# Reordering the emptying steps of a fused RWKV and FP4 feed-forward kernel: two rounding chains interleaved on VectorE

## What is computed

```python
attn = _rwkv_scan(r, k, v, w)                      # state = state*w + k v^T, out = state r
y = attn * g @ W_o.T
x = _layernorm(x + _layernorm(y) * ln_gamma + ln_beta)       # first two norms
def fp4_quant_dequant(x):                          # per block of 16
    scale = max(max(abs(xb)) / 6, 1e-12)
    return _GRID[searchsorted(_MID, abs(xb / scale))] * sign(xb) * scale
gate, up = fp4_linear(x, w_gate), fp4_linear(x, w_up)
h = silu(gate) * up                                # 704 hidden features
x = _layernorm(x + fp4_linear(h, w_down))          # third norm
```

## Time and profile before

| | us |
|---|---|
| median of 3 runs | 567.41 (565.97 to 568.02) |
| the profiled execution, its own time | 568.91 |
| its span | 567.00 |
| busy: PE / DVE / POOL / ACT | 520.9 / 508.8 / 286.1 / 260.0 |

### The profile page before, as it was taken

How to read it: one execution, slowest core, us unless ns; L and a number is a source line. 1 busy time by engine, 2 the same in 40 slices (tenths; PEclk the granted TensorE clock), 3 DMA queues, 4 the chain that set the end, 5 groups by cost and what they waited for, 6 DMA issues and landing times.

```text
span 567.0 us, 14892 instructions
## 1 busy us (share of the span) xinstructions
PE 520.9 (92%) x5169; PEld 453.7 (80%) x5169; DVE 508.8 (90%) x1535; ACT 260.0 (46%) x614; POOL 286.1 (50%) x439
## 2 busy tenths in 40 slices
PE   2769789899999999999999999999999999988775
PEld 1657568788888898988888888888988888867764
DVE  7998577999999999999999999999999999889983
ACT  3426454455444455445455544445544545432231
POOL 3246443445565555555554555555655545556232
PEclk9978789999999999999999999999999999999999
DMA  7300000000000000000000000000000000000001
GB/s 212 126 1 2 11 11 10 1 22 20 20 20 20 23 10 12 21 21 20 20 21 21 20 20 20 22 20 4 18 21 21 10 11 11 13 0 21 10 10 32
DMA packets 14046, 13.14 MB, mean 23 GB/s; under 512 B 2576, under 2 KB 13712, under 8 KB 13968
## 3 DMA queue, kind: packets, MB, share of 16 engines
q1 hardware_dynamic: 13968, 12.13, 7.0%
HBM read 7.93 MB, written 4.19 MB: 21 GB/s over the span
## 4 chain that ended last, share of the span: by engine, by line
issue 47%; POOL 40%; PE 5%; DVE 4%; ACT 2%; POOLq 1%; DMA 0%; ACTq 0%; DVEq 0%
POOL scores L410 11%; POOL rstd L392 11%; POOL hq L462 8%; POOL nmr L404 4%; POOL shift L435 3%; POOL xb L448 2%; DVE mix L1233 1%; POOL xq L419 1%; PE bank L794 1%; ACT scores L589 1%; PE bank L919 1%; PE bank L891 1%; PE bank L971 1%; PE bank L743 0%; PE bank L862 0%
## 5 line engine op out<-in xcount | busy, mean ns | idle before, releaser
L589 ACT COPY scores<-bank 128x512 f32<-128x512 f32 x128 | 68.3, 593 | 74.2 <-PE bank L794 74.2
L462 POOL TENSOR_TENSOR hq<-late,h_scale 128x704 f32<-128x704 f32 x31 | 43.2, 1392 | 96.4 <-DVE late L1092 96.4
L971 PE MATMUL bank<-down_t,hq_t 128*128 128x256 f32 x384 | 88.2, 379 | 0.9 <-ACT hq_t L665 0.8
L410 POOL TENSOR_SCALAR_AFFINE_SELECT scores<-scores 128x512 f32<-128x512 f32 x128 | 80.6, 666 | 11.2 <-ACT scores L589 11.2
L1233 DVE SCALAR_TENSOR_TENSOR mix<-shift,mu,x_t 128x128 f32<-128x128 f32 x256 | 80.9, 364 | 1.3 <-POOL shift L435 1.3
L971 PEld LDWEIGHTS bank<-down_t,hq_t 128*128 128x128 f32 x384 | 71.6, 190 | 9.6 <-issue 1.0
L419 POOL TENSOR_TENSOR xq<-x_grid,x_scale 128x256 f32<-128x256 f32 x32 | 19.9, 620 | 113.7 <-DVE x_grid L1092 113.7
L392 POOL TENSOR_TENSOR rstd<-veps,neg_half 128x1 f32<-128x1 f32 x96 | 65.2, 688 | 18.1 <-DVE veps L1180 18.0
L855 PE MATMUL bank<-gu_hi,xq_hi 128*128 128x352 f32 x256 | 71.2, 359 | 2.6 <-DVE late L1297 2.6
L891 PE MATMUL bank<-mix,proj_t 128*128 128x128 f32 x512 | 65.2, 281 | 0.1
L891 PEld LDWEIGHTS bank<-mix,proj_t 128*128 128x128 f32 x512 | 60.2, 193 | 3.5 <-issue 1.3
(11 more groups left out here) (130 smaller groups left out, 1145.1 us busy)
## 6 DMA issues: line engine op xcount, KB each, us to landing
x_tok<-in_L_attn_x_dram SPq DMA_DIRECT2D x32, 128.0 KB, 2.3
out_dram<-late_down SPq DMA_DIRECT2D x32, 128.0 KB, 1.7
late_down<-in_L_ffn_w_down_dram SPq DMA_DIRECT2D x1, 704.0 KB, 8.3
late<-in_L_ffn_w_gate_dram SPq DMA_DIRECT2D x1, 640.0 KB, 4.6
late<-in_L_ffn_w_up_dram SPq DMA_DIRECT2D x1, 640.0 KB, 6.9
scores<-in_L_attn_W_r_dram SPq DMA_DIRECT2D x1, 256.0 KB, 4.5
scores<-in_L_attn_W_v_dram SPq DMA_DIRECT2D x1, 256.0 KB, 4.6
scores<-in_L_attn_W_g_dram SPq DMA_DIRECT2D x1, 256.0 KB, 4.8
```

What stands on the lines that cost most here:

```text
L410: g.affine_select(out=a, in_=a, compare_op=ALU.is_ge, fill=0.0, base=0, pattern=[[0, 4], [1, P]], channel_multiplier=-1).then_inc(s_masked, 1)
L462: g.tensor_tensor(blocks(hq[:, t.c % 2, 0:HID], nb), blocks(h_grid, nb), per_block(h_scale, nb), ALU.mult).then_inc(hq_ready, 1)
L589: s.copy(scores[:, t.c % 2, 4 * q:4 * q + 4, :], src).then_inc(s_moved, 1)
L971: mm = t_.matmul(B_PA[:, 0:C], hq_t[:, t.c % 2, j], down_t[:, j], start=(j == 0), stop=(j == NH - 1))
```

## The change

Only the emptying steps' lists change, and one wait. On VectorE the x chain's links now stand between the h chain's, two or three places behind, and `gated(0)` moves from behind the norms to a place behind the sixth link of the h chain. Its wait is loosened to match: it asked for all seven links of the tile ahead, and now asks for four, since the fourth is the last that reads `hid`. `norm3` and the state update move back a little. On GpSimd, in emptying steps, `xq` moves from the end of the list to the place right behind `hq`, the second norm's rstd and nmr follow it, and the third norm's come last.

```diff
--- before.py
+++ after.py
@@ -461,6 +461,11 @@
                     nb = HID // BLK
                     g.tensor_tensor(blocks(hq[:, t.c % 2, 0:HID], nb), blocks(h_grid, nb),
                                     per_block(h_scale, nb), ALU.mult).then_inc(hq_ready, 1)
+                if drain:
+                    scale_x(tile(5), general)
+                    t = tile(4)
+                    if t is not None:
+                        rstd_of(t, 1, general)
                 t = tile(7 + ffn)
                 if t is not None and drain:
                     rstd_of(t, 2, general)
@@ -475,9 +480,9 @@
                                         per_block(h_scale[:, half * nb:(half + 1) * nb], nb), ALU.mult
                                         ).then_inc(last_ready, 1)
                 t = tile(4)
-                if t is not None:
+                if t is not None and not drain:
                     rstd_of(t, 1, general)
-                if not general:
+                if not general and not drain:
                     scale_x(tile(5), general)
                 if general:
                     scale_x(tile(4), general)
@@ -1291,7 +1296,7 @@
                     if t5 is None:
                         return
                     if i == 0:
-                        wait(dve, hquant_step, t5.count(QN, 0))
+                        wait(dve, hquant_step, t5.count(QN, 4 - QN))
                     wait(dve, gu_done, t5.count(2, i + 1))
                     wait(dve, sig_ready, t5.count(2, i + 1))
                     v.tensor_tensor(hid[:, i * HH:(i + 1) * HH], sig_h[:, i], B_UP[:, 0:HH], ALU.mult
@@ -1409,33 +1414,36 @@
                     norm1(0)
                     hgrid(1)
                     norm1(1)
+                    xgrid(0)
                     hgrid(2)
                     norm1(2)
+                    xgrid(1)
                     centred()
+                    xgrid(2)
                     low_x()
                     hgrid(3)
                     residual()
+                    xgrid(3)
+                    hgrid(4)
+                    xgrid(4)
                     gate_heads()
-                    hgrid(4)
                     if t2 is None:
                         add_x1()
+                    hgrid(5)
+                    xgrid(5)
+                    gated(0)
                     norm2(0)
-                    hgrid(5)
+                    hgrid(6)
+                    norm2(1)
                     norm3(0)
-                    norm2(1)
-                    hgrid(6)
+                    xgrid(6)
+                    norm2(2)
                     norm3(1)
-                    norm2(2)
+                    next_state(0)
                     norm3(2)
-                    next_state(0)
-                    gated(0)
+                    next_state(1)
                     last_grid(0)
-                    xgrid(0)
-                    next_state(1)
-                    xgrid(1)
                     next_state(2)
-                    for k in range(2, QN):
-                        xgrid(k)
                     gated(1)
                     last_grid(1)
                     return
```

## The result

The changed kernel takes 570.02 us (median of 6 runs, 569.52 to 571.15) beside 567.10 us of the kernel before (6 runs on the same chip): a ratio of 1.0048, with a 95% interval of 1.0033 to 1.0064. On the 567.41 us from which the prediction started that is 570.1, between 569.3 and 571.0. The forecast was 569.4, in a range of 567.4 to 571.0, with a chance of 0.74 on a change of under 0.5%; the ratio lies just within that, and its interval is clear of 1. So the total came out well, in part because two errors cancel. One thing that the prediction carried over unchanged, TensorE's clock, did not hold in the profiled execution, and the largest term of the sum, rightly sized, turned out to stand for something else.

A forecast was written before the change was run, and what follows sets the result against it. The prediction saw VectorE busy in almost all of the first four emptying steps. Its terms, -2.6 - 0.6 + 0.3 + 4.0 + 0.2 + 0.7 = +2.0 us on the 567.41 median, gave 569.4 us, range 567.4 to 571.0.

The forecast's parts named there:

- 53 to 54: Sign that the forecast is right: emptying steps 1 to 5 together take 53 to 54 us.
- bare links: x chain, steps 1 to 4: 22 links directly following their predecessor stop paying 0.12 us each, -2.6 us.
- second link: x chain's second link leaves the time of GpSimd's hq: three times 0.36 - 0.17, -0.6 us.
- hold: Steps 1 to 4: x's last link stands still beside GpSimd's hq, 1.0 us lost per step, +4.0 us.
- x1: Next step's x chain waits for x1, ready near 4.0 us after the h chain's end: +0.2 us, bounds 0 and 1.2.
- not held: Rival: x's last link is not held beside hq, waiting for x1 partly replaces the stall; 568.5 us, chance 0.12.
- +0.3: Step 2: the x and h chains' second links come into the time of GpSimd's four masks, costing +0.3 us.
- The rival with +3.4: Step 2: three VectorE instructions are held beside GpSimd's work, 1.7 us rather than 0.3; 570.8 us, chance 0.17.
- The ring: Step 5: early gating waits for PE's projections, which need hq; 7.9 instead of 7.28 us, with xq_lo +0.7.
- I carry their 17.28 us over: The last two steps, from 549.72 on, keep their order and so their 17.28 us.
- The rule of the Trainium skill: Rival: VectorE empties its pipe anyhow, so waiting links cost nothing extra and bare links save 0; 572.0 us, chance 0.03.
- The faster rival, 564.2: VectorE alone sets the pace, GpSimd does not hold it, x1 and the ring are in time: -3.2 us, chance 0.04.

The follow-up runs named there:

- the second kernel of experiment 7: The changed kernel with eight idle TensorE transposes ahead of its wait for hq, from the second emptying step on; 1.0041 of the kernel before.
- experiment 2: The changed kernel with x's last link, in emptying steps 2 to 4, taking its second operand from PSUM instead of SBUF; 1.0035 of the kernel before.
- experiment 4: The changed kernel's GpSimd order with a new VectorE order: h chain leading, x's last link behind the norm's pieces; 563.16 us, 0.9913 of the kernel before.
- experiment 5: The changed kernel with the first gating back behind the last norm of the step; 1.0129 of the kernel before.

## Why the prediction was right, and where not

The execution with the clock at 1.00 in all five steps (the second kernel of experiment 7) shows the prediction's own steps best, since on VectorE and GpSimd it is the changed kernel. Its five steps take 53.34 us, 1.94 more than the earlier trace rows; forecast were 2.0, and "53 to 54". In the profiled execution of the changed kernel they take 54.35, outside. That 1.94 lies so near 2.0 is in part luck: step 2 was put 0.5 too high and step 5 0.4 too low.

- *Steps 1, 3 and 4.* By the terms of bare links, second link, hold and x1 they were to be longer by 0.5, 0.1 and about 0.3 us; measured 0.49, 0.16 and 0.27. Of the x links only the third of step 4 is still bare: it starts at 534.37, 0.04 behind the end of the link ahead.
- *The last link of x: size right, meaning wrong.* 1.00, 0.99, 0.99 and 1.08 us of hold, 4.1 in all against 4.0. But in the sum the hold is a loss of its own. Its own rival "not held" saw that a wait for `x1` of 0.9 to 1.2 would replace it, and gave 568.5; experiment 2, with the hold gone from three of the four steps, shows waits of 0.81 and 1.15, a step 5 longer by 0.95 where the rival had 0.5, and 1.0035, which is 569.4. Most of the hold lies inside a time that the end of `hq` sets. That an earlier `hq` would take away most of hold and wait together was not seen at all, and it is worth some 4 us for one line (0.9968 against 1.0048; the five steps 49.52 against 53.34 at an equal clock).
- *Step 2.* Forecast +0.4, measured -0.09. The step that failed is the "+0.3" for the meetings with the masks: the holds beside the masks did occur (h's and x's second links 0.42 and 0.50 us against 0.17 for a free one), but VectorE waits 0.51 us for the rstd behind the masks in either kernel, so that holds ahead of that wait cost nothing. The other 0.2 is a wait of VectorE for TensorE ahead of `attn`, 0.20 in the kernel before, which is gone. The rival with +3.4 falls with the +0.3.
- *Step 5.* Forecast 7.9 (to 8.2), measured 8.39. The ring is as described, and it was summed too short: from the end of the h chain the first gating came 8.01 us later (540.59 to 548.60), not 7.6, and the terms given add up to 7.52. Of the 0.49 between, 0.26 is the time from the start of gate and up's second half (548.34) to the gating, which the sum left out; the transposes took 0.06, the down projection 0.08, and the copy with the gaps between the engines 0.08 more.
- *The clock.* "I carry their 17.28 us over", and the steps at a clock of 1.00, failed in the profiled execution: +0.53 in the rest (clock 0.85 against 0.93) and +1.01 in step 4. With the change TensorE's idle time moves from the wait for `xq` to the wait for `hq`. The prediction does not speak of that, and asked nothing about the clock.
- *Waits cost something.* The rule of the Trainium skill ("VectorE: DVE Perf Modes", section "The DRAIN you can't avoid") would have given 572.0, outside the measured 569.3 to 571.0. It agrees neither with this nor with the earlier trace rows. The section also says that a next instruction which is not held starts earlier, which the prediction left out; with that the start 0.08 ahead of an end in the earlier trace rows agrees. The faster rival, 564.2, named two conditions, and both were shown to fail: the link was held, and without the hold `x1` was late.

## What to carry to other kernels

Before an instruction that is held up, or a wait that comes in its place, is priced as the loss, look for what ends last behind it: two edits that each took the hold away won nothing that the runs can tell. GpSimd's queue could not go on before the long instruction had ended, and most of the time came back as waits. Start the long instruction earlier and fill its time with work that it does not hold; against the changed kernel one line moved that way was worth 0.8% here and an order made by it 1.3% (0.9968 and 0.9913 against 1.0048). And when two chains are interleaved, look at what stood between them as a cover: here the gating had to move with them (1.0129 without that).

## What the runs showed of the hardware that was not expected

The hold of a two-input VectorE instruction beside GpSimd's `hq` hangs on both operands being in SBUF: with one of them in PSUM the same link took 0.40 us inside `hq` instead of 1.41. If its own 0.42 us is taken from its end, the held one gets going 0.14 us before GpSimd's instruction ends. Which engine stands still follows the starts: with the division 0.03 ahead of GpSimd's addition, in experiment 4, the addition took 1.45 us instead of 0.72 and the division 0.88 instead of 1.46. TensorE's granted clock fell to 0.50 for some 3 us behind waits for `hq` of 1.0 to 1.7 us, in some of the profiled steps and not in others, and behind waits of 1.8 to 4.0 us for a bank in experiment 5; behind waits for `xq` of 1.53 to 1.55 us, as in the kernel before, the clock stayed at 1.00 in every step.
